# The first stage of a language-model tower on one core: key sums with one SBUF operand, and a new order of statistics, gathers and splits

## The reference, cut to what matters

```
h     = table[token_id]                        # gather, 256 floats a row
x     = (h - mean(h)) / sqrt(var(h) + 1e-5)    # layernorm
ct_q  = x @ Wd_q + b ;  ct_kv = x @ Wd_kv + b
query = ct_q  @ Wu_q + b + rope(ct_q @ Wq_r + b)
key   = ct_kv @ Wu_k + b + rope(x    @ Wk_r + b)
value = ct_kv @ Wu_v + b
rope(x0, x1) = (x0*cos - x1*sin,  x1*cos + x0*sin)     # even and odd columns
```

## Time and profile before

| what | value |
|---|---|
| median of 3 runs | 3316.14 us (3315.4 to 3316.4) |
| the profiled execution | 3315.87 us, its span 3314.0 us |
| stage A in it | 0 to 284 us |
| chunks in steady state, one by one | 16.0 us each |
| PE, DVE, ACT, POOL busy in the span | 97%, 88%, 74%, 17% |
| DMA in stage A | 82 to 105% of its 16 engines' time, 250 to 300 GB/s |

### The profile page before, as it was taken

The page is one execution under the profiler, slowest core; times in us unless marked ns, Lnnn a source line. Parts: engine busy times, 40 slices in busy tenths (PEclk is TensorE's granted clock), DMA queues, the critical chain, the costliest instruction groups (busy, mean ns, idle before and its releaser), DMA issues.

```text
span 3314.0 us, 67613 instructions
## 1 busy us (share of the span) xinstructions
PE 3202.7 (97%) x27520; PEld 1369.7 (41%) x27520; DVE 2908.6 (88%) x3157; ACT 2468.7 (74%) x4578; POOL 565.3 (17%) x752
## 2 busy tenths in 40 slices
PE   7997999999999999999999999999999999986999
PEld 3443333333333333333333333333333333365666
DVE  6889999999999999999999999999999999567222
ACT  3331888888888888888888888888888888943221
POOL 7882000000000000000000000000000000046233
PEclk9997999999999999999999999999999999998999
DMA  6895213131313131313131313122222220168773
GB/s 201 256 299 159 54 49 72 37 72 37 72 38 72 38 74 38 72 40 72 37 72 39 83 34 79 39 70 44 65 45 58 45 83 21 37 204 305 231 238 101
DMA packets 269155, 305.40 MB, mean 92 GB/s; under 512 B 45270, under 2 KB 198399, under 8 KB 265517
## 3 DMA queue, kind: packets, MB, share of 16 engines
q1 hardware_dynamic: 256812, 271.63, 29.7%
q0 software_dynamic: 12032, 29.45, 2.7%
HBM read 165.81 MB, written 139.23 MB: 92 GB/s over the span
## 4 chain that ended last, share of the span: by engine, by line
PE 81%; ACT 4%; DVE 3%; issue 2%; POOL 1%; DMA 0%; another core or an unknown queue 0%; SPq 0%; POOLq 0%; DVEq 0%
PE ps_o L916 33%; PE ps_s L899 26%; PE ps_m L868 13%; ACT probs L1012 2%; PE ps_g L1592 2%; PE ps_y L1603 2%; PE ps_u L1592 2%; DVE max_parts L1027 2%; ACT weighted L992 1%; PE ps_td L1581 1%; ACT rows_c L1343 1%; POOL slot_rows L1257 0%; PE ps_s L883 0%; POOL shift_c L1234 0%; DVE stats_c L1377 0%
## 5 line engine op out<-in xcount | busy, mean ns | idle before, releaser
L1027 DVE TENSOR_REDUCE max_parts<-ps_m 128x2 f32<-128x1024 f32 x2048 | 2486.1, 1223 | 79.9 <-PE ps_m L868 71.5
L1012 ACT ACTIVATE probs<-ps_s 128x512 f32<-128x512 f32 x4096 | 2217.5, 597 | 312.3 <-PE ps_s L899 127.8
L868 PE MATMUL ps_m<-keys,queries 48*128 48x512 f32 x4096 | 1483.5, 453 | 17.1 <-DVE max_parts L1027 16.7
L899 PE MATMUL ps_s<-queries,keys 51*128 51x512 f32 x4096 | 1480.5, 447 | 9.5 <-ACT probs L1012 3.1
L916 PE MATMUL ps_o<-probs,vals 128*32 128x256 f32 x16384 | 1295.5, 391 | 0.0
L899 PEld LDWEIGHTS ps_s<-queries,keys 51*128 51x128 f32 x4096 | 610.5, 185 | 832.2 <-issue 785.2
L868 PEld LDWEIGHTS ps_m<-keys,queries 48*128 48x128 f32 x4096 | 595.4, 187 | 77.4 <-DVE max_parts L1027 50.2
L916 PEld LDWEIGHTS ps_o<-probs,vals 128*32 128x32 f32 x16384 | 329.4, 108 | 720.4 <-issue 699.0
L824 POOL TENSOR_TENSOR heads_out<-weighted,recip_rows 128x512 f32<-128x512 f32 x63 | 80.9, 1285 | 2147.4 <-DMA recip_rows<-recip_rows_dram 2147.4
L1663 DVE TENSOR_TENSOR hidden<-ps_u,silu 128x320 f32<-128x320 f32 x64 | 31.5, 492 | 127.4 <-PE ps_u L1592 101.6
L1639 ACT ACTIVATE silu<-ps_g 128x320 f32<-128x320 f32 x64 | 28.0, 438 | 134.1 <-PE ps_g L1592 82.8
(11 more groups left out here) (108 smaller groups left out, 1600.0 us busy)
## 6 DMA issues: line engine op xcount, KB each, us to landing
slot_rows<-empty SPq DMA_DIRECT2D x16, 1290.0 KB, 5.2
vext<-val SPq DMA_DIRECT2D x64, 256.0 KB
halves_q<-parts SPq DMA_DIRECT2D x64, 256.0 KB
halves_k<-parts SPq DMA_DIRECT2D x64, 256.0 KB
keys<-halves_k SPq DMA_DIRECT2D x32, 512.0 KB, 7.5
queries<-halves_q SPq DMA_DIRECT2D x128, 128.0 KB, 3.2
vals<-vext SPq DMA_DIRECT2D x32, 512.0 KB, 5.6
recip_rows<-recip_rows_dram SPq DMA_DIRECT2D x64, 256.0 KB
```

What stands on the lines that cost most here:

```text
L868: mm = pe.matmul(ps_m[m % 2][:, h, :], queries_r[par][rows, qt, p, t * P:(t + 1) * P], keys_r[par][rows, p, c * 512:(c + 1) * 512], start= ...
L899: pe.matmul(ps_s[bank][:], keys_r[par][rows, p, k * P:(k + 1) * P], queries_r[par][rows, qt, p, :], start=True, stop=True).then_inc(scores ...
L1012: act.activation(probs[:, n % RING, :], ps_s[bank][:], ACT.Exp, scale=SCALE).then_inc(probs_ok[bank], 1)
L1027: dve.tensor_reduce(max_parts[:, lu % 2, :, p, t, c], ps_m[m % 2][:], AX.X, ALU.max).then_inc(maxima_ok[m % 2], 1)
```

## The change

Four things are rearranged in stage A.

1. Keys' terms. Of the keys' four rotary terms, the two with the sine are written back over `ps_r[:, 0:2]` in PSUM, the two with the cosine go to `terms_k` in SBUF. The keys' two sums on DVE then read one operand from SBUF and one from PSUM. So PE's next `rotary(.., 0)`, which writes `ps_r[:, 0:2]`, waits for those sums (`sums_ok[1]`) and no more for the terms (`terms_ok[1]`).
2. Statistics. Variance + eps and minus the mean go from POOL to DVE (`root_inputs`, two `tensor_scalar`). `row_moments` and `root_inputs` of the chunk two ahead stand right behind the queries' terms; `row_stats` is now of the chunk three ahead and stands between the keys' sums and the keys' content.
3. POOL. The gather stands in front of the queries' sums. `root` follows the sums. The keys' rest of a chunk (L404 with x = 1, now `rest(.., 1)`) is taken one chunk later, behind the root; ACT's rounding of it moves likewise.
4. PE. The next chunk's transposes stand behind the queries' rotary part, in front of their content (not in chunk 0).

SP's list is not touched. Stage C has memsets counted on the same semaphore as stage A's; as two memsets go (`eps_sb`, `no_mean` of stage A), its wait is for 4 instead of 6.

```
             def rest(b, k, x):
+                pool.wait_ge(high_ok[x], after(b, k))
+                pool.tensor_tensor(parts[:, k % 2, x, 1].bitcast(F32R), full[:, x], parts[:, k % 2, x, 0], ALU.subtract).then_inc(low_ok[x], 1)
...
                     pool.wait_ge(norm_ok, b * (CPB * CT) + k * CT)
                     pool.wait_ge(emb_out[ahead[1]], ahead[0] * 16)
                     pool.wait_ge(ids_in[ahead[1]], ahead[0] * 16 + 16)
+                    gather(*ahead)
                 pool.wait_ge(terms_ok[0], after(b, k, 4))
...
-                if ahead:
-                    gather(*ahead)
-                for x in range(2):
-                    if x == 1 and not (last and k + 2 >= CPB):
...
-                    pool.wait_ge(high_ok[x], after(b, k))
...
+                if not (last and k + 2 >= CPB):
+                    root(*((b, k + 2) if k + 2 < CPB else (b + 1, k + 2 - CPB)))
+                if (b, k) != (0, 0):
+                    rest(*((b, k - 1) if k else (b - 1, CPB - 1)), 1)
+                rest(b, k, 0)
...
# PE
-                    pe.wait_ge(terms_ok[1], b * (CPB * 4) + k * 4)
+                    pe.wait_ge(sums_ok[1], b * (CPB * 2) + k * 2)
...
                 rotary(b, k, 0)
+                early = more and (b, k) != (0, 0)
+                if early:
+                    transpose(*nxt)
                 content(b, k, 0)
...
# ACT
+                if (b, k) != (0, 0):
+                    split(*((b, k - 1) if k else (b - 1, CPB - 1)), 1)
                 split(b, k, 0)
                 if more:
                     copy_lat(*nxt)
-                split(b, k, 1)
...
# DVE
+            def root_inputs(b, k):
+                dve.wait_ge(stats_ok, after(b, k, CT))
+                dve.tensor_scalar(neg_mean[:, k, :], mv[:, k, :, 0], -1.0, None, ALU.mult)
+                dve.tensor_scalar(var_eps[:, k, :], mv[:, k, :, 1], EPS, None, ALU.add).then_inc(eps_ok, 1)
...
+                    dsts = [terms_k[:, 0, :], ps_r[:, 0, :], terms_k[:, 1, :], ps_r[:, 1, :]]
...
+            def key_sums(b, k):
+                dve.wait_ge(terms_ok[1], after(b, k, 4))
+                dve.tensor_tensor(sums[:, 1, 0, :], terms_k[:, 0, :], ps_r[:, 1, :], ALU.subtract).then_inc(sums_ok[1], 1)
+                dve.tensor_tensor(sums[:, 1, 1, :], terms_k[:, 1, :], ps_r[:, 0, :], ALU.add).then_inc(sums_ok[1], 1)
```

More of the change, by code:

```diff
@@ L236, in phase_a @@
         lat = sb("lat", [P, 2, 2, CH])
-        terms = sb("terms", [P, 2, 4, CH])
+        terms = sb("terms", [P, 1, 4, CH])
+        terms_k = sb("terms_k", [P, 2, CH])
         sums = sb("sums", [P, 2, 2, CH])
@@ L410, in _ @@
                 chunk(BATCH - 1, k, True)
+            rest(BATCH - 1, CPB - 1, 1)
         @block.tensor
@@ L472, in chunk @@
                 rotary(b, k, 0)
+                early = more and (b, k) != (0, 0)
+                if early:
+                    transpose(*nxt)
                 content(b, k, 0)
                 values(b, k)
-                if more:
+                if more and not early:
                     transpose(*nxt)
@@ L555, in rope_terms @@
                     dve.wait_ge(sums_ok[0], b * (CPB * 2) + k * 2)
[L556 to L557 removed]
+                    dsts = [terms[:, 0, n, :] for n in range(4)]
+                else:
+                    dsts = [terms_k[:, 0, :], ps_r[:, 0, :], terms_k[:, 1, :], ps_r[:, 1, :]]
+                order = ((0, cos_sb), (1, sin_sb), (1, cos_sb), (0, sin_sb)) if x == 0 else \
+                        ((0, cos_sb), (0, sin_sb), (1, cos_sb), (1, sin_sb))
+                for dst, (eo, tab) in zip(dsts, order):
+                    dve.scalar_tensor_tensor(dst, ps_r[:, eo, :], b_cols[:, 2 + 4 * x + eo:3 + 4 * x + eo],
                                              tab[:, pos], ALU.add, ALU.mult).then_inc(terms_ok[x], 1)
+            def key_sums(b, k):
+                dve.wait_ge(terms_ok[1], after(b, k, 4))
+                dve.tensor_tensor(sums[:, 1, 0, :], terms_k[:, 0, :], ps_r[:, 1, :], ALU.subtract).then_inc(sums_ok[1], 1)
+                dve.tensor_tensor(sums[:, 1, 1, :], terms_k[:, 1, :], ps_r[:, 0, :], ALU.add).then_inc(sums_ok[1], 1)
             def add_content(b, k, x):
@@ L569, in _ @@
             dve.memset(val[:], 1.0).then_inc(ones_set, 1)
[L570 to L575, removed]
+            for k in range(2):
+                row_stats(0, k)
+                dve.wait_ge(stats_raw, (k + 1) * CT)
+                row_moments(0, k)
+                root_inputs(0, k)
             dve.wait_ge(const_in, 16 * NCONST)
@@ L581, in chunk @@
                 rope_terms(b, k, 0)
+                ahead = None if last and k + 2 >= CPB else (b, k + 2) if k + 2 < CPB else (b + 1, k + 2 - CPB)
+                if (b, k) == (0, 0):
+                    row_stats(*ahead)
+                if ahead:
+                    dve.wait_ge(stats_raw, after(*ahead, CT))
+                    row_moments(*ahead)
+                    root_inputs(*ahead)
                 dve.wait_ge(val_out[k % 2], uses(b, k, CT * 16))
@@ L589, in chunk @@
                 add_content(b, k, 0)
[L590 to L593, removed]
                 rope_terms(b, k, 1)
[L595 to L599, removed]
+                key_sums(b, k)
+                third = None if last and k + 3 >= CPB else (b, k + 3) if k + 3 < CPB else (b + 1, k + 3 - CPB)
+                if third:
+                    row_stats(*third)
                 add_content(b, k, 1)
```

17 lines of the change are left out of this document (4 added, 13 removed).

## The result

| | before | after |
|---|---|---|
| median | 3316.27 us (4 runs, 3315.4 to 3317.53) | 3357.77 us (4 runs, 3355.43 to 3365.11) |
| profiled execution, its span | 3315.87, 3314.0 us | 3357.48, 3355.7 us |
| start of stage B (first `max_parts`) | 284.2 us | 324.7 us |
| from there to the end of the span | 3029.8 us | 3031.0 us |

The change makes the kernel slower: ratio 1.0128, 95% interval 1.0115 to 1.014. The forecast was 3356 us. Of the 41.7 us between the two spans, 40.5 lie in stage A.

What follows compares the result with a forecast made beforehand. No engine full; the changed kernel bound by a POOL and emb_rows store loop, 11.0 + 7.5 = 18.5 us a chunk. Start +1.6, chunks 2 to 12 +40.9, end -1.3 and -0.7: +40.5 on 3315.87, 3356 us; range 3332 to 3372.

Steps and rivals of the forecast that it cites:

- The loop: POOL's gather to SP's emb_rows store landing and the next gather: 11.0 + 7.5 = 18.5 us a chunk, bounds 17.0 and 19.3.
- POOL's leg: POOL from gather through sums, root and shift, and the previous chunk's keys' rest: 11.0 us, with nothing waiting.
- second leg: SP's queue, from low_ok[1] to the landing of the emb_rows store: 7.5 us, lower bound 6.04.
- Part 1: Keys' terms on DVE: first sum from 2.11 to 0.66 us, PSUM writes cost nothing; alone, 14.66 us a chunk.
- Part 2: Statistics: two tiny instructions more on DVE, 0.2 to 0.4 us a chunk, counted as nothing in the loop.
- Part 4: Earlier transposes on PE: nothing sooner that anyone waits for, over 3 us idle a chunk in the loop; cost nothing.
- The loads of stage B: In SP's queue before the rows' store: +10.4 us behind chunk 6, +3.0 each behind chunks 7, 9 and 10.
- The end: Chunks 12 to 15, without gathers: PE sets 44.0 us against 45.3, -1.3; last sums free of POOL, -0.7.
- 1: Rival: store lands before POOL asks, no closed loop, chunks 14.66 us, 3301 us in all; 0.06 together with 4.
- 2: Rival: landing of the emb_rows store takes only 5.0 us, loop equals the earlier 16.0; 3325 us; chance 0.03.
- 3: Rival: PE's clock stays low after each chunk's gap, PE exceeds the loop by some 2 us; 3380 us; chance 0.05.
- 4: Rival: as 1, but POOL's sums block DVE's tensor_scalar, 0.4 us a chunk, 3305 us; 0.06 together with 1.

Runs made afterwards that it cites:

- e1: Changed kernel, but SP issues the ids and emb_rows store of the next chunk before its wait for low_ok[1]; 3308.9 us, ratio to before 0.9977.
- e2: Changed kernel, but the next chunk's ids and emb_rows store follow SP's wait for low_ok[1] directly, ahead of the keys' stores; 3308.6 us, ratio to before 0.9977.
- e7: Changed kernel with the keys' rest and ACT's rounding of it back in their own chunk, gather still first; 3362.1 us, ratio to before 1.015.
- e3: Kernel before with only the keys' terms changed (two in PSUM) and PE waiting for the sums; 3301.1 us, ratio to before 0.9952.
- e8: e1 with variance + eps and minus the mean back on POOL, without DVE's two tensor_scalar; 3297.8 us, ratio to before 0.9951.
- e6: Changed kernel with POOL's gather and its waits moved back behind the queries' sums; 3331.9 us, ratio to before 1.0051.
- e10: e5 with the next chunk's transposes back behind the values on PE; 3297.0 us, ratio to before 0.9942.
- e5: e1 with the next chunk's ids and emb_rows store at the start of SP's chunk, before the values' stores; 3293.8 us, ratio to before 0.9935.
- e9: Kernel before with the keys' terms changed as in e3 and SP's order of e5, nothing else; 3302.0 us, ratio to before 0.9947.

## Why the prediction was right

- **The loop** (part 3), on which all rested: POOL's leg 10.9 us against 11.0; signal to landing 7.6 against 7.5; the chunk 18.5 as forecast. e1 and e2 show that it is this loop that sets the chunk, and e7 that its DMA wait needs the deferred rest. The two pieces of the second leg were each a little off: SP's queue had moved 1.58 MB by 116.2, 6.2 us after the signal (6.3 forecast), and POOL started about 1.4 us after that (1.2 forecast from the earlier trace rows). The Trainium skill's 2 us ("DMA: Bandwidth & Descriptors", Anatomy of one DMA), put in place of the 1.2, would have made the leg 8.3. The plain legs are all 7.6, and 1.4 is nearer to 1.2; but the page states the figure for DMAs issued by POOL and counts the setup with it, so this SP store is no test of it.
- **Part 1**: 0.69 us where 0.66 was forecast, a PSUM write 0.75 against 0.74. Alone it gives the 14.7 us a chunk that the prediction named (e3).
- **Part 2** counted as nothing: its two new instructions, 0.17 and 0.16 us in the loop, cost nothing (e8). That the statistics' new place depends on the early gather (e6) was not seen.
- **Part 4** counted as nothing: true in the loop, 0.17 us a chunk outside it (e10).
- **The loads of stage B**: behind chunk 6 +10.8 against +10.4. Behind chunks 7, 9 and 10 the second leg was 9.6 to 9.7 and not 10.5, the steps +2.0 to +2.1 and not +3.0. Against that the steps to chunks 7 and 10 took 1.4 and 0.9 us more than a plain one, which was not foreseen. These errors cancel, so that the 204.3 us from chunk 2 to 12 against 204.4 flatters the forecast.

  What was late in those two is the landing: no load of stage B stands in them, yet their second legs are 9.0 and 8.5 us (signals at 147.03 and 216.83, gathers at 155.99 and 225.31), and the rows' store needs 5.1 and 4.6 us from issue to landing, 3.7 in a plain chunk. Of the eleven second legs these two alone hold a packet of the queue named `instruction` with 0.02 MB. From the DMA view of 147.03 to 155.99:

```profile
q8 instruction: 1, 0.02, 0.7%
...
emb_rows<-emb SPq DMA_DIRECT2D x1, 512.0 KB, 5.1
```

  That this packet holds the store up is likely and not shown.
- **The end**: chunk 12 to 15 43.8 us against 44.0. Stage A ends 40.5 us later, as the sum had it.
- **Rivals**: 1 is what a chunk would be with an early store (e1: 14.63 us, against 14.66; its total of 3309 is still above the rival's 3301); the changed kernel is not that, since its SP list puts the store behind the signal. 2 and 3 are out: the landing was not 5.0, and although some rotary parts ran slow (3.16 us in the row above, 1.98 in the next chunk), the chunks kept 18.5, and no matmul of the keys' rotary part took over 0.60 us. 4 is half right. In e1, timeline:

```profile
150.00 1.26 POOL L396 TENSOR_TENSOR sums<-terms 128x512 f32<-128x512 f32 x1 [1.26 <-DVE terms L571]
150.24 1.06 DVE L557 TENSOR_SCALAR neg_mean<-mv 128x4 f32<-128x4 f32 x1
...
151.21 0.16 DVE L558 TENSOR_SCALAR var_eps<-mv 128x4 f32<-128x4 f32 x1
```

This is one chunk of e1. DVE's first `tensor_scalar` on four elements a partition starts 0.24 us into POOL's sum and lasts until that ends, 1.06 us; the second takes 0.16. By the rule of the Trainium skill ("SBUF — State Buffer", Who interferes with whom) one side fully blocks, and this trace agrees. The price forecast for it, 0.4 us a chunk, is wrong: e8, without them, has the same chunk.

## What to carry to other kernels

Before a wait moves earlier in one engine's list, follow what it waits for through the other queues: here the store stood in an in-order DMA list behind a signal that the waiting engine itself gives later, and a wait with a chunk of slack became a loop of 18.5 us. The cure was in the queue: move the store that frees a ring slot in front of the waits and bulk stores that it doesn't need (e5, 20 us below before). Test parts of a change alone, since here one part was worth 15 us and the others nothing or less.

## What the runs showed of the hardware

- A `tensor_scalar` of DVE on four elements a partition takes 0.16 to 0.17 us alone, 1.06 in the row above beside a POOL operation.
- DVE's key sum of two SBUF operands takes 2.11 us beside POOL's rest and 0.66 alone; with one operand in PSUM it takes 0.66 to 0.69 beside the rest too (e3, changed kernel).
- A rotary term (128x512, one operand in PSUM, the table in SBUF) takes DVE 0.75 us when it is written to PSUM, 0.74 when written to SBUF.
- Four stores whose issue takes about 4 us in plain chunks took SP 12.8 and 13.0 us behind the four queued key loads (e1, e5): the issuing queue is held up as well as the transfers.
- The low clock at the start of stage B lasted 40 us longer in one profiled execution (e9) than in two others, in the same instructions, and that execution spent 18 us more behind stage A than the kernel before did, most of it there. What sets its length stays open.
